# A mixture-of-experts layer: shared expert in 384 and 320 features, slot table turned one step sooner, last scatters awaited by SyncE

## The chip, the cores and the metric

The kernel runs on one core of a Trainium2 chip. The metric is the device time of one execution in microseconds (us). Three executions of the kernel before took 974.53, 976.37 and 980.57 us; the median is 976.37 us. One further execution was profiled, and all rows and times of engines come from it.

## What is computed

Inputs are x (4 x 512 tokens of 512 features), normalised per token to xn. Three things are added to x: an attention stand-in (projection, a scan over the tokens, projection), a routed mixture of experts and a shared expert:

```python
d = sigmoid(decay)
projected = xn @ W_in.T
state_t = d * state_(t-1) + (1 - d) * projected_t        # per sequence
attn = states @ W_out.T + bias

scores = softmax(xn @ wg_router.T)                        # 32 experts
topk_w, topk_idx = top_k(scores, 6);  topk_w /= sum(topk_w)
y  = sum over the 6 chosen e: topk_w * (silu(xn @ w_gate[e]) * (xn @ w_up[e])) @ w_down[e]   # F = 352
sh = (silu(xn @ ws_gate) * (xn @ ws_up)) @ ws_down                                            # 2F = 704
out = x + attn + y + sh
```

Matrix products are done to nearly float32 precision with three passes of TensorE: an operand is split into a high part (rounded to the fast format fp32r) and a low part (the rest), and hi*hi + hi*lo + lo*hi is accumulated.

## The kernel before, in words

**Units.** After the attention part, which ends at about 137 us, TensorE works through 40 units. Units 0 to 7 are the shared expert: SH = 8, two units for each of the four sequences, tokens() = 512. An even unit does features 0 to 351 of the shared expert, an odd one 352 to 703. Units 8 to 39 are the routed experts in order of load, with 448 down to 360 slots each. Every unit has three chunks of features, c = 0, 1, 2, of 128, 128 and 96 (FLAST). The order of TensorE in unit u is written out by hand: gate_up(u, 0), down(u-1, 2), gate_up(u, 1), down(u, 0), gate_up(u, 2), down(u, 1). A waiting instruction holds all that stands behind it on its engine.

**Cost of a chunk in matmuls.** For c = 0 and 1, gate and up are 4 slices of D times 3 passes each, so 24 matmuls. For c = 2 (gate_up_last), the first 64 gate and 64 up features stand in one 128-wide operand (WIDE_GU, 12 matmuls). The last 32 gate and 32 up features stand in another with their high and low parts side by side (w_nar, NARROW_GU), which needs only 2 passes: 8 matmuls (narrow). down is 3 matmuls for each of 4 blocks of tokens and each chunk, 12 per chunk. A shared unit has 24 + 24 + 20 + 36 = 104 matmuls, each 512 columns.

**ScalarE and VectorE** turn a chunk into the operand of down: silu (ScalarE), mult (VectorE), h_hi (ScalarE), h_lo (VectorE). For c = 2 it is silu, wide_h, and for the narrow part narrow_low (ScalarE), narrow_sum (VectorE), silu_narrow (ScalarE), narrow_h (VectorE) ahead of h_hi and h_lo. Three PSUM banks p_gu are used in turn. Weights come to raw (two halves), ScalarE writes the high part (w_hi_piece) and VectorE the low part (w_lo_piece), in pieces GATE, UP, WIDE_GU, NARROW_GU, DOWN, counted in s_wh and s_w.

**Slot table.** While units 0 to 5 run, GpSimd sends 96 small scatters (send, L582) that write which token has which slot of which expert. VectorE computes the places of choice k (choice_slots) in unit k-1. GpSimd then loads the table to tabrow (L593, L594). TensorE turns it (table_T, 4 small transposes) in unit 6 behind gate_up(6, 2). VectorE copies it out at the end of unit 6 (table_out, L1612 to L1616). Only then can GpSimd gather the tokens of units 8 and 9 (gather, L599). Their rows are rearranged by DMAs issued from SyncE and ScalarE (quarters, L369), transposed by VectorE (squares, L1571) and split (xt_hi, xt_lo) before unit 8's first matmul. ScalarE issues 8 of these DMAs in unit 7, between w_hi_piece(8, UP) and silu of chunk 1.

**Routed loop.** GpSimd gathers for unit u+2 once unit u+1's operand is split, then scatters unit u-1's result into out (scatter, L613). ScalarE evacuates y of unit u-1 (y_out) between pieces of unit u's work.

**End.** GpSimd issues the last three scatters, waits until all have landed (s_scat), reads a count (value_load, L641), branches over a loop for extra blocks that is not entered here, and meets the other engines at the end of the block (L123).

## Time and profile before

| what | value |
|---|---|
| median of three executions | 976.37 us (974.53 to 980.57) |
| the profiled execution, its own time | 976.6 us |
| its span, first to last instruction | 974.6 us |
| TensorE busy | 931.4 us (96% of the span) |
| VectorE, ScalarE, GpSimd busy | 651.6, 498.3, 516.9 us |
| mean granted clock of TensorE | 0.985 of 2.4 GHz |

The span is 2.0 us shorter than the execution's own time. Busy times of a matmul overlap with the next one's, because matmuls are pipelined: what a matmul costs in a stream is read from start to start.

### The profile page before, as it was taken

To read this page: it belongs to the slowest core of one execution; us is meant where nothing else is said; L and a number is where in the kernel's file an instruction comes from. 1 tells how busy PE (TensorE), PEld (TensorE's weight loads), DVE (VectorE), ACT (ScalarE), POOL (GpSimd) and SP (SyncE) were. 2 spreads that over 40 slices of the span, in tenths; PEclk is the share of its full clock that TensorE was granted. 3 is DMA by queue.
4 is the path that set the end of the run, shared out by engine and by line. 5 is a ranking of instruction groups with operands and counts; after the bars stand their busy time and mean duration, and the time that the engine had idled before them with its cause. 6 is when DMAs were issued, how large, how long until landed. Compare 5 with 4: busy or idle time off the path is not lost.

```text
span 974.6 us, 14045 instructions
## 1 busy us (share of the span) xinstructions
PE 931.4 (96%) x4596; PEld 836.7 (86%) x4596; DVE 651.6 (67%) x1098; ACT 498.3 (51%) x853; POOL 516.9 (53%) x376
## 2 busy tenths in 40 slices
PE   6899979999999999999999999999999999999992
PEld 6798868888888888899999999999999899989891
DVE  6789987454533676877667766776677667667650
ACT  5543224222222355766566756676566566566641
POOL 6210257777740435656665666566547547546341
PEclk9899989999999999999999999999999999999996
DMA  9506236130232559999998998989999989999842
GB/s 331 165 1 218 87 110 206 38 88 1 87 97 90 145 192 295 252 226 217 227 247 244 227 233 216 285 214 221 246 258 239 252 245 249 255 246 245 207 55 37
DMA packets 125834, 182.59 MB, mean 187 GB/s; under 512 B 19012, under 2 KB 72900, under 8 KB 125760
## 3 DMA queue, kind: packets, MB, share of 16 engines
q1 hardware_dynamic: 97840, 126.14, 41.7%
q0 software_dynamic: 26704, 55.01, 28.1%
q8 instruction: 38, 0.62, 0.3%
q10 hardware_dynamic: 1216, 0.53, 0.2%
q14 instruction: 36, 0.29, 0.1%
HBM read 114.21 MB, written 40.85 MB: 159 GB/s over the span
## 4 chain that ended last, share of the span: by engine, by line
PE 55%; DMA 11%; DVE 10%; SPq 8%; issue 7%; POOL 5%; ACT 3%; ACTq 1%; POOLq 0%; DVEq 0%
PE p_gu L961 10%; PE p_gu L962 10%; PE p_gu L963 10%; SPq L369 8%; DMA xnT<-xn_rows,ids 7%; PE p_y L961 6%; PE p_y L962 6%; PE p_y L963 6%; DMA xnT<-xnT 3%; POOL xnT L599 3%; POOL out L613 2%; DVE w_lo L1214 2%; PE p_gu L1045 2%; PE p_gu L1043 2%; DVE scan L1475 1%
## 5 line engine op out<-in xcount | busy, mean ns | idle before, releaser
L613 POOL DMA_INDIRECT out<-rows,ids x112 | 204.0, 1822 | 221.4 <-ACT rows L672 197.0
L961 PE MATMUL p_gu<-xT_hi,w_hi 128*128 128x512 f32 (+12 forms) x800 | 280.5, 351 | 0.6 <-DVE xT_lo L1214 0.6
L963 PE MATMUL p_gu<-xT_hi,w_lo 128*128 128x512 f32 (+12 forms) x800 | 280.4, 351 | 0.0
L962 PE MATMUL p_gu<-xT_lo,w_hi 128*128 128x512 f32 (+12 forms) x800 | 280.3, 350 | 0.0
L599 POOL DMA_INDIRECT xnT<-xn_rows,ids x112 | 164.5, 1468 | 88.6 <-issue 33.3
L1214 DVE TENSOR_TENSOR w_lo<-raw,w_hi 128x1024 fp32r<-128x1024 f32 (+2 forms) x134 | 161.3, 1205 | 0.5 <-ACT w_hi L672 0.5
L961 PEld LDWEIGHTS p_gu<-xT_hi,w_hi 128*128 128x128 f32 x800 | 150.2, 188 | 12.0 <-DVE xT_lo L1214 1.0
L962 PEld LDWEIGHTS p_gu<-xT_lo,w_hi 128*128 128x128 f32 x800 | 150.3, 188 | 10.9
L963 PEld LDWEIGHTS p_gu<-xT_hi,w_lo 128*128 128x128 f32 x800 | 150.3, 188 | 7.2
L961 PE MATMUL p_y<-w_hi,hT_hi 128*128 128x512 f32 (+1 forms) x384 | 151.5, 395 | 4.9 <-DVE hT_lo L1214 2.0
L962 PE MATMUL p_y<-w_lo,hT_hi 128*128 128x512 f32 (+1 forms) x384 | 150.5, 392 | 0.0
L963 PE MATMUL p_y<-w_hi,hT_lo 128*128 128x512 f32 (+1 forms) x384 | 150.2, 391 | 0.0
L672 ACT ACTIVATE w_hi<-raw 128x1024 fp32r<-128x1024 f32 (+2 forms) x136 | 142.6, 1051 | 7.6 <-PE p_y L963 6.3
L1420 DVE TENSOR_TENSOR h_sb<-sg,p_gu 128x512 f32<-128x512 f32 (+12 forms) x80 | 46.0, 574 | 127.3 <-PE p_gu L963 110.9
L582 POOL DMA_INDIRECT slot_table<-pay,slot_i x96 | 107.3, 1117 | 34.0 <-issue 27.7
L716 ACT ACTIVATE sg<-p_gu 128x512 f32<-128x512 f32 (+24 forms) x120 | 61.6, 513 | 120.2 <-PE p_gu L963 111.9
L672 ACT ACTIVATE hT_hi<-h_sb 128x384 fp32r<-128x384 f32 (+9 forms) x120 | 64.7, 540 | 112.5 <-DVE h_sb L1420 86.1
L1214 DVE TENSOR_TENSOR hT_lo<-h_sb,hT_hi 128x384 fp32r<-128x384 f32 (+9 forms) x120 | 68.9, 574 | 33.4 <-ACT hT_hi L672 32.8
L961 PEld LDWEIGHTS p_y<-w_hi,hT_hi 128*128 128x128 f32 (+1 forms) x384 | 72.1, 188 | 21.9 <-ACT rows L672 3.9
L1571 DVE STREAM_TRANSPOSE xT_raw<-xnT 128x512 f32<-128x512 f32 x112 | 72.9, 652 | 23.6 <-DMA xnT<-xnT 23.6
L672 ACT ACTIVATE xT_hi<-xT_raw 128x512 fp32r<-128x512 f32 (+3 forms) x112 | 64.9, 580 | 40.6 <-DVE xT_raw L1571 38.9
L963 PEld LDWEIGHTS p_y<-w_hi,hT_lo 128*128 128x128 f32 (+1 forms) x384 | 72.1, 188 | 15.7
(190 smaller groups left out, 1218.4 us busy)
## 6 DMA issues: line engine op xcount, KB each, us to landing
raw<-L_ffn_w_gate SPq DMA_DIRECT2D x32, 704.0 KB, 5.8
raw<-L_ffn_w_up SPq DMA_DIRECT2D x32, 704.0 KB, 7.8
xnT<-xnT SPq DMA_DIRECT2D x424, 48.0 KB
raw<-L_ffn_w_down SPq DMA_DIRECT2D x32, 512.0 KB
out<-rows SPq DMA_DIRECT2D x28, 256.0 KB, 3.3
xring<-L_attn_x SPq DMA_DIRECT2D x24, 256.0 KB, 3.6
raw<-L_ffn_w_down SPq DMA_DIRECT2D x32, 192.0 KB
xnT<-xnT SPq DMA_DIRECT2D x80, 64.0 KB
```

What stands on the lines that cost most here:

```text
L369: queue.dma_start(xq[par][a_ * SQ:(a_ + 1) * SQ, 0:n, b, :], xe[b * SQ:(b + 1) * SQ, 4 * par:4 * par + n, a_ * P:(a_ + 1) * P]).then_inc(s ...
L582: pool.indirect_dma_start(out=table[:, :], in_=pay[:, c, :], in_offset=None, out_offset=bass.IndirectOffsetOnAxis(ap=slot_i[:, c:c + 1], a ...
L599: pool.indirect_dma_start(out=xe[0:n, 4 * (u % 2) + t, :], out_offset=None, in_=xn_rows[:, :], in_offset=bass.IndirectOffsetOnAxis(ap=ids[ ...
L613: pool.indirect_dma_start(out=out[:, :], in_=y_sb[t][0:n, :], in_offset=None, out_offset=bass.IndirectOffsetOnAxis(ap=ids[0:n, col:col + 1 ...
L672: return a.activation(dst, src, ACT.Copy, scale=scale)
L716: a.activation(sg[0:k, 0:n], p_gu[2 * q % 3][0:k, 0:n], ACT.Silu).then_inc(s_sg, 1)
L961: t_.matmul(dst, stat[0], mov[0], start=first, stop=False)
L962: t_.matmul(dst, stat[0], mov[1], start=False, stop=False)
L963: return t_.matmul(dst, stat[1], mov[0], start=False, stop=last)
L1214: return v.tensor_tensor(dst, src, hi, ALU.subtract)
L1420: v.tensor_tensor(h_sb[0:k, 0:n], sg[0:k, 0:n], p_gu[(2 * q + 1) % 3][0:k, 0:n], ALU.mult).then_inc(s_h, 1)
L1571: v.transpose(xT_raw[u % 2][:, :, t * P:t * P + n].rearrange("p s (b j) -> p b s j", j=SQ), xq[u % 2][:, t, 0:n // SQ, :].rearrange("p b ( ...
```

## The change

The 704 features of the shared expert are cut into 384 and 320 instead of 352 and 352.

- An even unit has three full chunks of 128. Its chunk 2 has gate in one operand (in the place of WIDE_GU) and up in another: high part in w_nar[:, 0], low part in w_nar[:, 1]. It is 24 matmuls, and is followed by plain silu and mult.
- An odd unit has chunks of 128, 128 and 64. Its chunk 2 is WIDE_GU alone, 12 matmuls, then silu and wide_h. h_lo writes the low part of h to partitions 64 to 127 of hT_hi, under the high part, and the last 64 rows of ws_down are loaded twice, to partitions 0 to 63 and 64 to 127. down(u, 2) of an odd unit is then 2 matmuls per block: high and low part of h at once against the high weights, and the high part of h against the low weights.
- Set 0 of shared weights is 18 KB per partition in raw, so two scratch tiles move by 1 KB. One memset of raw and two waits on it go.
- table_T moves from behind gate_up(6, 2) to behind down(5, 2) in unit 6, and table_out on VectorE from the end of unit 6 to behind shared_out, ahead of the mult of chunk 1.
- GpSimd's wait for all scatters goes inside the branch that is not entered; SyncE waits for them as its last instruction.

The core of the diff (counters of semaphores, which follow from the above, are left out):

```diff
-KF = (P, P, FLAST)
+FS_EVEN = FC * P
+FS_ODD = 2 * F - FS_EVEN
...
+def width(u):
+    return F if u >= SH else (FS_EVEN, FS_ODD)[u % 2]
+def kf(q):
+    return min(P, width(q // 3) - q % 3 * P)
+def full_last(u):
+    return u < SH and u % 2 == 0
+def wide_only(u):
+    return u < SH and u % 2 == 1
...
             def shared_set(s):
...
+                down = shared_down(s).rearrange("p (c d) -> p c d", d=D)
+                sp.dma_start(down[:, 0:FC - 1, :],
+                             ws_down[a:a + FULL, :].rearrange("(c p) d -> p c d", p=P)
+                             ).then_inc(s_ld[2][0], 16)
+                for at_ in range(0, P, f - FULL):
+                    sp.dma_start(down[at_:at_ + f - FULL, FC - 1, :], ws_down[a + FULL:a + f, :]
+                                 ).then_inc(s_ld[2][0], 16)
...
             def gate_up_last(u):
...
                     mm = three(p_gu[2 * q % 3][:, 0:n], wide_pass(u % 2, kc),
                                [x_hi[:, kc, 0:n], x_lo[:, kc, 0:n]], kc == 0, kc == DC - 1)
+                if wide_only(u):
+                    mm.then_inc(s_ud, 1)
+                    return
                 mm.then_inc(s_gd, 1)
...
                 pe.wait_ge(s_sg, q)
+                if full_last(u):
+                    for kc in range(DC):
+                        mm = three(p_gu[(2 * q + 1) % 3][:, 0:n], [w_nar[:, i, kc, :] for i in range(2)],
+                                   [x_hi[:, kc, 0:n], x_lo[:, kc, 0:n]], kc == 0, kc == DC - 1)
+                    mm.then_inc(s_ud, 1)
+                    return
                 narrow(p_gu[(2 * q + 1) % 3], u % 2, (x_hi, x_lo), n).then_inc(s_ud, 1)
...
             def down(u, c):
...
+                    elif wide_only(u) and last:
+                        t_.matmul(p_y[t][:], hT_hi[:, q % 2, t * P:(t + 1) * P],
+                                  w_hi[:, u % 2, lo:lo + D], start=False, stop=False)
+                        mm = t_.matmul(p_y[t][:], hT_hi[0:k, q % 2, t * P:(t + 1) * P],
+                                       w_lo[0:k, u % 2, lo:lo + D], start=False, stop=True)
...
                 if u > 0:
                     down(u - 1, 2)
+                if u == SH - 2:
+                    table_T()
                 gate_up(u, 1)
                 down(u, 0)
                 gate_up(u, 2)
-                if u == SH - 2:
-                    table_T()
                 down(u, 1)
...
             def h_lo(q):
...
-                    low(hT_lo[0:k, q % 2, 0:n], h_sb[0:k, 0:n], hT_hi[0:k, q % 2, 0:n]
-                        ).then_inc(s_ht, 1)
+                    dst = hT_hi[WIDE:P] if k == WIDE else hT_lo[0:k]
+                    low(dst[:, q % 2, 0:n], h_sb[0:k, 0:n], hT_hi[0:k, q % 2, 0:n]).then_inc(s_ht, 1)
...
                         shared_out(t)
+                if u == SH - 2:
+                    table_out()
...
-                wide_h(u)
+                if full_last(u):
+                    mult(3 * u + 2)
+                else:
+                    wide_h(u)
                 if split is not None:
                     w_lo_piece(split, DOWN)
-                narrow_sum(u)
-                narrow_h(u)
+                if u >= SH:
+                    narrow_sum(u)
+                    narrow_h(u)
                 h_lo(3 * u + 2)
-                if u == SH - 2:
-                    table_out()
...
             scatter(UNITS - 1)
-            pool.wait_ge(s_scat, 16 * XB_ALL)
...
             more = pool.value_load(cnt_i[0:1, 0:1], min_val=0, max_val=XMAX)
             with pool.If(more > 0):
+                pool.wait_ge(s_scat, 16 * XB_ALL)
...
             more = sp.value_load(cnt_i[0:1, 0:1], min_val=0, max_val=XMAX)
             with sp.If(more > 0):
...
+            sp.wait_ge(s_scat, 16 * XB_ALL)
```

## Rows read from the trace of the kernel before

**Rows 1.** Busy time by stretch: TensorE, its weight loads, VectorE, ScalarE, GpSimd, granted clock.

```profile
core 0: us, PE busy (x) PEld busy (x) DVE busy (x) ACT busy (x) POOL busy (x), PEclk, DMA share, GB/s
137.00:336.00 199.00, 199.00 (x876) 164.02 (x874) 104.64 (x158) 55.96 (x82) 119.42 (x111) 1.00 0.34 100
336.00:650.00 314.00, 311.68 (x1544) 286.67 (x1544) 224.06 (x386) 196.53 (x363) 190.77 (x118) 1.00 0.89 232
...
765.00:912.00 147.00, 145.24 (x770) 133.92 (x769) 103.49 (x156) 93.13 (x155) 81.64 (x48) 1.00 0.97 251
```

**Rows 2.** Instructions in time, VectorE then TensorE, late in the routed units.

```profile
908.54 0.71 DVE L1571 STREAM_TRANSPOSE xT_raw<-xnT 128x512 f32<-128x512 f32 x1 [2.77 <-DMA xnT<-xnT]
...
911.59 0.47 PE L961 MATMUL p_y<-w_hi,hT_hi 128*128 128x512 f32 x1 [0.42 <-ACT rows L672]
```

**Rows 3.** TensorE in time, unit 1: its first matmul, narrow's first, unit 2's first.

```profile
169.42 0.39 PE L961 MATMUL p_gu<-xT_hi,w_hi 128*128 128x512 f32 x1
...
188.51 0.39 PE L1043 MATMUL p_gu<-xT_hi,w_nar 128*128 128x512 f32 x1
...
193.04 0.39 PE L961 MATMUL p_gu<-xT_hi,w_hi 128*128 128x512 f32 x1
```

**Rows 4.** TensorE in time around table_T and in units 7 and 8.

```profile
295.74 0.40 PE L961 MATMUL p_gu<-xT_hi,w_hi 128*128 128x512 f32 x1
...
308.47 0.26 PE L1142 MATMUL p_tx<-ident,tabrow 112*128 112x112 f32 x1
...
333.24 0.39 PE L961 MATMUL p_y<-w_hi,hT_hi 128*128 128x512 f32 x1
...
335.73 0.39 PE L963 MATMUL p_y<-w_hi,hT_lo 128*128 128x512 f32 x1
336.71 0.47 PE L961 MATMUL p_gu<-xT_hi,w_hi 128*128 128x448 f32 x1 [0.59 <-DVE xT_lo L1214]
...
342.60 0.50 PE L961 MATMUL p_y<-w_hi,hT_hi 96*128 96x512 f32 x1 [0.76 <-DVE hT_lo L1214]
...
351.15 0.47 PE L961 MATMUL p_y<-w_hi,hT_hi 128*128 128x512 f32 x1 [0.66 <-DVE rows L1603]
```

**Rows 5.** GpSimd in time: scatters of choices 4 and 5, load of the table.

```profile
235.31 0.98 POOL L582 DMA_INDIRECT slot_table<-pay,slot_i  x1 [1.80 <-DVE slot_i L1398]
...
258.93 0.98 POOL L582 DMA_INDIRECT slot_table<-pay,slot_i  x1 [1.19 <-DVE slot_i L1398]
...
283.31 0.63 POOL L593 DMA_DIRECT2D tabrow<-slot_table  x1 [3.32 <-DMA slot_table<-pay,slot_i]
283.93 0.59 POOL L594 DMA_DIRECT2D tabrow<-slot_table  x1
```

**Rows 6.** The tile tabrow: from issue to landing of its two loads.

```profile
DMA to landing us min/median/max: 5.4/5.7/6.1
```

**Rows 7.** Gathers, rearranging DMAs and silu in time: GpSimd, then ScalarE.

```profile
314.68 1.09 POOL L599 DMA_INDIRECT xnT<-xn_rows,ids  x1 [30.16 <-DVE wts L1616]
...
322.30 6.13 ACTq L369 DMA_DIRECT2D xnT<-xnT  x8
...
328.53 0.60 ACT L716 ACTIVATE sg<-p_gu 128x512 f32<-128x512 f32 x1 [8.20 <-issue]
```

**Rows 8.** VectorE in time: units 6 and 7.

```profile
301.46 0.69 DVE L1420 TENSOR_TENSOR h_sb<-sg,p_gu 128x512 f32<-128x512 f32 x1 [3.74 <-issue]
...
330.55 0.69 DVE L1214 TENSOR_TENSOR hT_lo<-h_sb,hT_hi 128x512 fp32r<-128x512 f32 x1 [0.70 <-ACT hT_hi L672]
...
335.66 0.99 DVE L1214 TENSOR_TENSOR xT_lo<-xT_raw,xT_hi 128x512 fp32r<-128x512 f32 x2
```

**Rows 9.** The end: GpSimd's last scatter, its read of the count, the block's end.

```profile
961.41 1.61 POOL L613 DMA_INDIRECT out<-rows,ids  x1 [0.30 <-issue]
...
L641 POOLq TENSOR_LOAD <-cnt_i x1: 516/516/516, 966.9 to 966.9; - x1
...
L123 SPq DRAIN  x1: 7/7/7, 921.1 to 921.1; - x1
...
L123 POOLq DRAIN  x1: 6358/6358/6358, 968.0 to 968.0; - x1
```

More of the change, by code:

```diff
@@ L348, in split_part, with from_raw, to_split @@
             return w[:, s, W_DOWN:W_ALL]
+        def from_raw(u, piece):
+            n = weight_set(u)
+            return shared_part(n, piece) if n < 2 else raw_part(raw_half(n), piece)
+        def to_split(w, u, piece):
+            if full_last(u) and piece == WIDE_GU:
+                return w[:, 0, W_WIDE:W_DOWN].rearrange("p (c f) -> p c f", c=DC)
+            if full_last(u) and piece == NARROW_GU:
+                return w_nar[:, 0 if w is w_hi else 1]
+            return split_part(w, u % 2, piece)
         def x_tile(t):
@@ L379, in tile_rows, with load_set @@
                 return dram[bass.ds(P * t, P), :]
-            def load_set(h, split, g_src, u_src, d_src):
+            def load_set(h, before, g_src, u_src, d_src):
                 for j, src in ((0, g_src), (1, u_src)):
-                    if split is not None:
-                        sp.wait_ge(s_w, split + NARROW_GU + 1)
+                    if before is not None:
+                        sp.wait_ge(s_w, split_done(before, DOWN) - 1)
                     lo, hi = PIECES[j]
@@ L387, in load_set @@
                                  ).then_inc(s_ld[j][h], 16)
-                if split is not None:
-                    sp.wait_ge(s_w, split + DOWN + 1)
+                if before is not None:
+                    sp.wait_ge(s_w, split_done(before, DOWN))
                 lo, hi = PIECES[2]
@@ L683, in w_hi_piece @@
                     act.wait_ge(s_dd if j == DOWN else s_ud, 3 * (u - 1))
-                copy(split_part(w_hi, u % 2, j), raw_part(half, j)).then_inc(s_wh, 1)
+                copy(to_split(w_hi, u, j), from_raw(u, j)).then_inc(s_wh, 1)
             def normalise(t):
@@ L712, in silu @@
                     act.wait_ge(s_pre, 64)
-                act.wait_ge(s_gd, q + 1)
+                u = q // 3
+                if wide_only(u) and q % 3 == FC - 1:
+                    act.wait_ge(s_ud, q + 1)
+                else:
+                    act.wait_ge(s_gd, gate_done(q))
                 act.wait_ge(s_h, q)
-                n, k = tokens(q // 3), (P, P, WIDE)[q % 3]
+                n, k = tokens(u), P if full_last(u) else (P, P, WIDE)[q % 3]
                 a.activation(sg[0:k, 0:n], p_gu[2 * q % 3][0:k, 0:n], ACT.Silu).then_inc(s_sg, 1)
@@ L731, in h_hi @@
                 act.wait_ge(s_h, q + 1)
[L732 to L734 removed]
+                if q % 3 == 2 and q >= 3 * SH:
+                    act.wait_ge(s_he, rank_of(q // 3) + 1)
+                n, k = tokens(q // 3), kf(q)
                 if ends_half(q // 3):
@@ L877, in _ @@
                 if split is not None:
-                    w_hi_piece(split, NARROW_GU)
+                    if not wide_only(split):
+                        w_hi_piece(split, NARROW_GU)
                     w_hi_piece(split, DOWN)
@@ L885, in _ @@
                 silu(3 * u + 2)
-                narrow_low(u)
-                silu_narrow(u)
+                if u >= SH:
+                    narrow_low(u)
+                    silu_narrow(u)
                 h_hi(3 * u + 2)
@@ L894, in _ @@
                 with act.Fori(0, more) as k:
-                    for j in range(3):
-                        act.wait_ge(s_ld[j][0], (2 if j == 2 else 1) * 16 * (k + raw_loads(E) + 1))
+                    for j in (0, 1):
+                        act.wait_ge(s_ld[j][0], 16 * (k + raw_loads(E) + 1))
+                    act.wait_ge(s_ld[2][0], 32 * k + 16 * (down_loads(E) + 2))
                     act.wait_ge(s_dd, 3 * k + 3 * UNITS)
@@ L1658, in _ @@
                     w_lo_piece(split, WIDE_GU)
-                    w_lo_piece(split, NARROW_GU)
+                    if not wide_only(split):
+                        w_lo_piece(split, NARROW_GU)
                 if early is not None and blocks(early) > 3:
```

138 lines of the change are left out of this document (85 added, 53 removed).

## The prediction

> **What bounds the kernel now.** I first read the table of busy time by stretch. From 137 to 336 us, the shared units, TensorE is busy in all of 199.00 us, at a granted clock of 1.00, while VectorE works 104.64 and ScalarE 55.96 us [rows 1]. So in this stretch time is the number of matmuls times their pitch, and other engines matter only where they make TensorE wait. In the routed units TensorE is idle for 2.32 us of 314 and 1.76 us of 147 [rows 1]: it is the bound there too, though late in the run only just. There the loop of gather, rearranging DMA and transpose is nearly as slow: VectorE stood 2.77 us before a transpose for a DMA, and 0.42 us of that kind of delay came through to TensorE [rows 2]. I then read TensorE in order of time for its pitch [rows 3] and for the places where it does stop [rows 4], then the producers behind those places [rows 5 to 8], and last the end [rows 9].
>
> **Fewer matmuls.** Unit 1 takes 193.04 - 169.42 = 23.62 us for 104 matmuls, so the pitch is 0.227 us [rows 3]. An even unit goes from 104 to 108 (chunk 2 from 12 + 8 to 24), an odd one to 92 (8 fewer in gate_up, 4 fewer in down). A pair saves 8, four pairs save 32: 32 x 0.227 = 7.27 us. Narrower operands cost the same: the pitch of unit 1 holds 96-row ones already. This is the term that I am surest of, since there is no idle time here to hide it.
>
> The row gives 0.227 us from start to start. The Trainium skill (TensorE: Matmul & The Clock Gate, Back-to-back issue gap) states about 131 ns per matmul as the sustained rate of a stream of weight loads and matmuls at 512 columns. The trace disagrees; by that figure 32 matmuls would be worth 4.2 us, and the forecast would be 3.1 us higher.
>
> **Is each operand ready for the earlier matmuls?** Shifts of TensorE against before, in matmuls: +4 behind gate_up(0, 2), -8 behind each whole pair; 24 (5.45 us) at the place of table_T in unit 6; 20 (4.54 us) in the first two chunks of unit 7; 28 (6.36 us) at the start of unit 8. The tightest place is chunk 1 of an odd unit, whose down comes 8 matmuls (1.8 us) sooner. In unit 7, where ScalarE is held by issuing DMAs, its hT_lo ended at 330.55 + 0.69 = 331.24 and down began at 333.24 [rows 4, 8], 2.0 us of margin; how it changes is worked out below. In other odd units ScalarE issues no DMAs, so their margin is larger. Behind chunk 2 the odd unit's down(u, 2) stands 24 matmuls later (5.4 us), and the chain there loses four instructions (narrow_low, narrow_sum, silu_narrow, narrow_h), while the even unit loses them too. I cost it at nothing. The split of set 0 has 256 columns more on each of the two engines and that of set 1 as many fewer: nothing, beside a busy TensorE. The removed memset and waits stand near the start, where GpSimd is not the bound: nothing, at most a few tenths.
>
> **The table turned sooner.** The 4 transposes are moved and not removed. TensorE reaches them at 295.74 - 5.45 = 290.3 [rows 4]. It then needs the table to have landed. Before, the loads were issued at 283.31 and 283.93 and took up to 6.1 us [rows 5, 6]: 290.0. GpSimd waited 1.80 and 1.19 us for choices 4 and 5 [rows 5], of which 0.30 stands before any scatter; VectorE comes to choice 4 sooner by 4 matmuls (0.9 us) and to choice 5 by 16 (3.6 us), but to choice 2 by 4 later. I take 1.5 us sooner for the load (bounds 0 and 2.4). The table lands near 288.5, 1.8 us before it is needed; at the bound of 0 the margin is 0.3. Behind table_T stands all of TensorE, so each microsecond of lateness would cost one: bounds 0 and 2 us, taken at 0. table_out now stands before mult of unit 6's chunk 1, where VectorE had been idle 3.74 us [rows 8]; its six small instructions fit. If that cover were gone, h of chunk 1 would be late.
>
> The first gather started at 314.68, after 30.16 us of waiting for the table's copy [rows 7]. It can start near 294, so tokens of units 8 and 9 are there long before they are asked for. What was late next: ScalarE was free at 328.53 - 8.20 = 320.33, stood until 322.30 for the gathers, and issued 8 DMAs in 6.13 us, and only then did silu [rows 7]. Now it issues from 320.33 - 4.54 = 315.8 to 321.9. From silu's start to the last xT_lo (336.65) was 8.12 us [rows 7, 8], so that one ends at 330.1. In the same way hT_lo of chunk 1 ends 2.71 us after silu's start, at 324.7, against a down at 333.24 - 6.36 = 326.9: no stop. TensorE reaches unit 8 at 336.71 - 0.75 - 6.36 = 329.6 (the 0.75 is 336.71 - 335.73 less a pitch [rows 4]) and waits 0.5 us. Gain 0.25 us (bounds -0.75, +0.75, by how long the 8 issues take).
>
> Next, down(7, 2) waited 0.76 us for hT_lo [rows 4], whose chain ran through the narrow steps behind the transposes; each took about as long as its neighbours (0.60 and 0.69 us [rows 7, 8]), so the chain is some 2.6 us shorter and the wait goes: gain 0.75 us (bounds 0 and 0.76). Then down(8, 0) waited 0.66 us for shared_out [rows 4], in VectorE's queue behind the transposes of unit 9. VectorE is less late now, but this queue is full: I take half, 0.3 us (bounds 0 and 0.66). After that everything is shifted alike. gather(10) waits for unit 8's operand and comes 6.5 us sooner, TensorE 8.6 us.
>
> **The end.** GpSimd's last scatter is done at 963.02. It waits for landing until 966.9, reads the count, and its DRAIN starts at 968.0 and takes 6.36 us: the kernel ends with it at 974.4 [rows 9]. In the changed kernel GpSimd doesn't wait. The 1.1 us from read to DRAIN start at 963.0, the DRAIN at 964.1, and it ends at 970.5, beside the landing instead of behind it. SyncE, idle since 921.1, sees the landing at 966.9 and its DRAIN is 7 ns [rows 9]. Gain 3.85 us, if the DRAIN's length is its own. No row shows a GpSimd DRAIN with DMAs in flight: bounds 0 (it counts from the landing, and the reading is not saved either) and 7.6 (it vanishes). I take the length in the row, since no DMA was in flight when it ran.
>
> That drain has a rule against it, which is the rival below. The Trainium skill (VectorE: DVE Perf Modes, The DRAIN you can't avoid) gives drains at a kernel's borders as about 12 ns on all engines. SyncE's 7 ns agrees, GpSimd's 6358 ns doesn't.
>
> **Sum.** 7.27 + 0.25 + 0.75 + 0.3 + 3.85 = 12.4 us. The profiled execution took 976.6 us (span 974.6), so **964.2 us** (span 962.2). The median of before, 976.37, is 0.2 us away: the sum holds for it too.
>
> **Rivals.**
> - *The drain starts anew at the landing.* For it: we don't know what 6.36 us consist of. Against: it ran when nothing was left to land. The end then gives 1.1 us (the reading) or 0: 967.0 to 968.0 us. Chance 0.17.
> - *The drain shrinks* to what SyncE's takes, and the end is the landing: 974.5 - 966.9 = 7.6 us from the end, 960.4 us. Chance 0.05.
> - *The gather loop takes over.* gather(10) comes only 6.5 us sooner against TensorE's 8.6. If the loop sets the late units, which VectorE's 2.77 us speak for and TensorE's 0.42 us against [rows 2], TensorE ends with 6.5 + 3.85: 966.2 us. Chance 0.12.
> - *The odd units don't get shorter*, because TensorE waits for h instead. Then the 16 matmuls that even units gain cost 3.6 us, and only the end is won: 976.4 us. The margin of 2 us at the tightest place [rows 4, 8] is against it. Chance 0.06.
> - *Slower: table_T holds TensorE.* It pays from a landing later than 290.3 us, one for one, and turns the sign 12.4 us later, at 302.7: a load of 20 us where 5.4 to 6.1 were seen [rows 6]. To be 1% slower it needs over 30 us. Chance 0.03, with anything else of this sign.
>
> **How the numbers follow.** My forecast has 0.57; the rivals have 0.43. About 1% is what a measurement of this kernel can tell from no change, that is 966.6 and 986.1 us. Faster by over 1%: the forecast 0.57, less 0.03 for its upper end, the shrunk drain 0.05, most of the loop case 0.09, and a little of the new-start drain 0.03: 0.71. Slower by over 1%: 0.03. Within: 0.26. The range goes down to 961.0 (the upper bounds of the start of unit 8 and a drain that starts during the last scatter) and up to 968.5, which takes in the loop case and the drain that starts anew, and leaves out the shrunk drain, the waiting odd units and the slower case, less than 0.2 together.
>
> **What would show it.** Right: 108 and 92 matmuls in shared units at a pitch of 0.227 us, no gap in TensorE between 137 us and unit 8, unit 8's first matmul near 330.2, table_T near 290.3 with no wait, the first gather near 294, TensorE's last matmuls some 8.6 us sooner, and GpSimd's DRAIN at about 6.4 us, starting before the scatters land. Wrong: a wait before table_T, a wait for hT_lo in units 1, 3, 5 or 7, longer gaps for rows after 765 us, or a DRAIN that ends as long after the landing as before.

## Result and the profile after

The changed kernel took 973.84 us (median of 20 executions, 969.61 to 980.05), the kernel before 976.29 us beside it (median of 20). The ratio is 0.9966, 95% interval 0.9951 to 0.9982: 2.45 us were won where 12.4 were forecast. The forecast of 964.2 us and its range (961.0 to 968.5) missed. The profiled execution took 976.52 us with a span of 974.8 us; that of before had 974.6. A single execution moves by 3 us and more, so times are taken from medians and places from profiles. Ratios compare the means of the executions that ran undisturbed, without those in a slower state, so a ratio and the quotient of two medians can differ by some tenths of a per cent.

**Down of the 64-feature chunk.** This is TensorE in order of time at the end of gate_up(5, 2) and through down(5, 2), which is directly ahead of table_T. Columns: start us, duration us, engine, line, operands, shapes, wait ahead. The operand that a weight load (PEld) puts into TensorE is here a block of hT_hi, not a weight of the model; both operands of such a matmul have the same number of rows. These eight matmuls are called a group below.

```profile
292.91 0.39 PE L1056 MATMUL p_gu<-xT_hi,w_lo 128*128 128x512 f32 x1
293.14 0.39 PE L1223 MATMUL p_y<-w_hi,hT_hi 128*128 128x512 f32 x1
293.45 0.50 PE L1225 MATMUL p_y<-w_lo,hT_hi 64*128 64x512 f32 x1
293.88 0.49 PE L1223 MATMUL p_y<-w_hi,hT_hi 128*128 128x512 f32 x1
294.31 0.50 PE L1225 MATMUL p_y<-w_lo,hT_hi 64*128 64x512 f32 x1
...
296.01 0.50 PE L1225 MATMUL p_y<-w_lo,hT_hi 64*128 64x512 f32 x1
296.44 0.37 PE L1254 MATMUL p_tx<-ident,tabrow 112*128 112x112 f32 x1
```

Up to 293.14 the pitch is the 0.227 us of [rows 3]. Then a matmul of 128 rows and one of 64 alternate, and each starts 0.43 us behind the last. Eight take 3.30 us instead of 1.81. No wait is shown ahead of any of them, and the clock did not fall during them, as the stretches below show. The weight loads (PEld) of the same stretch say what happens:

```profile
292.91 0.19 PEld L1223 LDWEIGHTS p_y<-w_hi,hT_hi 128*128 128x128 f32 x1
293.45 0.18 PEld L1225 LDWEIGHTS p_y<-w_lo,hT_hi 64*128 64x128 f32 x1 [0.35 <-issue]
293.88 0.19 PEld L1223 LDWEIGHTS p_y<-w_hi,hT_hi 128*128 128x128 f32 x1 [0.24 <-issue]
294.31 0.18 PEld L1225 LDWEIGHTS p_y<-w_lo,hT_hi 64*128 64x128 f32 x1 [0.24 <-issue]
```

The load for 293.14 was done under the matmul before it (292.91). From there on each load stands idle for 0.24 us and starts together with its own matmul: it no longer runs under the previous matmul. The waits of the weight loads over the whole run, in us, times and longest, show the same. The kernel before had four waits of this kind at p_y (3.3 us), as the changed kernel has at L1054; the other 28 are new:

```profile
PEld p_y L1225 <- issue: 4.3, 16, 0.4
...
PEld p_y L1054 <- issue: 4.1, 4, 1.6
...
PEld p_y L1223 <- issue: 2.9, 12, 0.2
```

**Clock.** The same stretches by window (columns as in [rows 1]: busy times, granted clock, DMA share, GB/s).

```profile
199.00:202.60 3.60, 3.60 (x11) 1.51 (x10) 2.38 (x4) 2.35 (x2) 2.92 (x3) 1.00 0.02 1
293.10:296.50 3.40, 3.40 (x10) 1.35 (x9) 2.41 (x4) 0.63 (x1) 0.00 (x0) 1.00 0.00 0
296.50:297.70 1.20, 1.20 (x5) 0.72 (x4) 1.20 (x3) 0.00 (x0) 0.00 (x0) 0.61 0.67 222
297.70:300.00 2.30, 2.30 (x6) 1.82 (x6) 1.33 (x7) 0.00 (x0) 0.12 (x1) 0.50 0.90 282
300.00:303.00 3.00, 3.00 (x8) 2.31 (x7) 0.00 (x0) 0.00 (x0) 2.39 (x3) 0.50 1.02 373
303.00:306.00 3.00, 3.00 (x13) 2.43 (x12) 0.00 (x0) 0.60 (x1) 2.39 (x3) 0.90 0.84 297
```

The slow groups run at 1.00. But behind this group and the four short transposes of table_T the clock is 0.50 (the 1.2 GHz level), and 13 matmuls run at 0.43 us, some 2.8 us lost. In the kernel before, nothing of the kind stood around table_T [rows 1, 4].

**Table and gathers, GpSimd.** The table is loaded at 283.81 and 284.43 (283.31 before [rows 5]), table_T starts at 296.44 with no wait, and the first gather is 14.8 us earlier than in [rows 7]:

```profile
283.81 0.63 POOL L678 DMA_DIRECT2D tabrow<-slot_table  x1 [2.48 <-DMA slot_table<-pay,slot_i]
284.43 0.59 POOL L679 DMA_DIRECT2D tabrow<-slot_table  x1
299.88 1.09 POOL L684 DMA_INDIRECT xnT<-xn_rows,ids  x1 [14.86 <-DVE wts L1727]
```

**Unit 8 and the routed loop.** All three waits of [rows 4] behind 335 us are gone, but unit 8 starts at 338.70, not near 330.2. TensorE there:

```profile
338.70 0.36 PE L1054 MATMUL p_gu<-xT_hi,w_hi 128*128 128x448 f32 x1
```

ScalarE in order of time at its first piece of unit 10's weights, in the kernel before:

```profile
364.76 1.06 ACT L672 ACTIVATE w_hi<-raw 128x1024 fp32r<-128x1024 f32 x1 [1.32 <-DMA raw<-L_ffn_w_gate]
```

The same piece after, then SyncE's queue, then TensorE, each in a fence of its own:

```profile
369.71 1.06 ACT L757 ACTIVATE w_hi<-raw 128x1024 fp32r<-128x1024 f32 x1 [5.67 <-DMA raw<-L_ffn_w_gate]
```

```profile
347.68 10.79 SPq L444 DMA_DIRECT2D xnT<-xnT  x16
358.51 2.21 SPq L547 DMA_DIRECT2D out<-rows  x4
362.12 0.36 SPq L461 DMA_DIRECT2D raw<-L_ffn_w_gate  x1
```

```profile
373.50 0.47 PE L1054 MATMUL p_y<-w_hi,hT_hi 128*128 128x512 f32 x1 [0.27 <-ACT rows L757]
...
376.39 0.50 PE L1054 MATMUL p_y<-w_hi,hT_hi 128*128 128x512 f32 x1 [1.26 <-ACT rows L757]
```

SyncE issues unit 10's weights behind 16 rearranging DMAs (10.79 us) and four stores. They come at 369.7, ScalarE stands for them 5.67 us (1.32 before) with its evacuations queued behind, and TensorE loses 1.5 us in two stops. TensorE had no stop here before.

**The end.** First GpSimd's last scatter, then, in the second fence, the lines of the block's end (count, duration in ns, start in us). SyncE's COMPARE_BRANCH carries its wait for the scatters, so its start, 969.9, marks their landing.

```profile
964.54 1.61 POOL L698 DMA_INDIRECT out<-rows,ids  x1 [0.30 <-issue]
```

```profile
L168 POOLq DRAIN  x1: 11561/11561/11561, 963.0 to 963.0; - x1
L168 SPq COMPARE_BRANCH  x1: 38/38/38, 969.9 to 969.9; - x1
L168 SPq DRAIN  x1: 67/67/67, 970.4 to 970.4; - x1
```

From the last scatter's end (966.15) to the DRAIN's end (974.56) are 8.41 us. Before they were 974.36 - 963.02 = 11.34 [rows 9]. So 2.9 us are won, not 3.85. The DRAIN ran from 963.0, beside the scatters, but it didn't end by itself: it took 11.56 us and ended 4.6 us behind the landing.

**A ledger.** Four stretches, each against the same stretch of before in the profiled executions: TensorE's first matmul of unit 0 (137.68 before), from there to unit 8 (199.03), from there to the last matmul (620.37), and on to the end of the span (17.5). The three kernels on the right are experiments, told of below. Each column is one execution, and that of the changed kernel was 2.7 us slower than its median; a stretch also moves by some 1 us between executions (the routed units of tail_only, an experiment that doesn't touch them, are 1.1 us shorter than before).

| us against before | forecast | after | full_rows_fifth | changed_early_load_again | full_rows_early_load |
|---|---|---|---|---|---|
| start of unit 0 | 0 | +1.4 | +2.9 | +4.0 | +3.5 |
| units 0 to 7 | -6.6 | +0.6 | -7.2 | -2.7 | -7.5 |
| routed units | -2.0 | +1.2 | +4.7 | -2.1 | -4.6 |
| end | -3.85 | -3.0 | -3.1 | -2.8 | -2.9 |
| span | -12.4 | +0.2 | -2.7 | -3.5 | -11.5 |

### The profile page after: what moved, and what is told of

Same layout as the page of the kernel before. It is cut to its first block, busy times and chain, and to the rows that moved or that the text cites. A ratio compares the mean times of both kernels' runs of the same rounds, so it can differ in the third digit from the quotient of the medians.

```text
span 974.8 us, 13932 instructions
## 1 busy us (share of the span) xinstructions
PE 936.7 (96%) x4564; PEld 836.8 (86%) x4564; DVE 641.8 (66%) x1081; ACT 488.6 (50%) x836; POOL 515.2 (53%) x375
## 4 chain that ended last, share of the span: by engine, by line
PE 68%; DVE 9%; DMA 6%; SPq 6%; issue 5%; POOL 3%; ACT 2%; ACTq 1%; POOLq 0%; DVEq 0%
PE p_gu L1054 13%; PE p_gu L1056 13%; PE p_gu L1055 13%; PE p_y L1054 7%; PE p_y L1055 7%; PE p_y L1056 7%; SPq L444 5%; DMA xnT<-xn_rows,ids 3%; DVE w_lo L1326 2%; DMA xnT<-xnT 2%; PE p_gu L1138 2%; POOL xnT L684 2%; PE p_gu L1136 2%; PE p_y L1040 1%; DVE scan L1586 1%
## 5 line engine op out<-in xcount | busy, mean ns | idle before, releaser
L1054 PE MATMUL p_gu<-xT_hi,w_hi 128*128 128x512 f32 (+12 forms) x800 | 282.2, 353 | 0.0
L684 POOL DMA_INDIRECT xnT<-xn_rows,ids x112 | 167.3, 1494 | 88.5 <-DVE xT_lo L1326 40.4
L1054 PEld LDWEIGHTS p_gu<-xT_hi,w_hi 128*128 128x128 f32 x800 | 151.0, 189 | 11.9 <-issue 0.7
L1531 DVE TENSOR_TENSOR h_sb<-sg,p_gu 128x512 f32<-128x512 f32 (+12 forms) x84 | 48.6, 579 | 158.2 <-PE p_gu L1056 144.4
L1054 PE MATMUL p_y<-w_hi,hT_hi 128*128 128x512 f32 (+1 forms) x368 | 144.7, 393 | 5.8 <-ACT rows L757 4.2
L757 ACT ACTIVATE w_hi<-raw 128x1024 fp32r<-128x1024 f32 (+2 forms) x136 | 142.6, 1050 | 11.9 <-PE p_y L1056 6.3
L1055 PE MATMUL p_y<-w_lo,hT_hi 128*128 128x512 f32 (+1 forms) x368 | 144.2, 392 | 0.0
L1056 PE MATMUL p_y<-w_hi,hT_lo 128*128 128x512 f32 (+1 forms) x368 | 144.0, 391 | 0.0
L805 ACT ACTIVATE sg<-p_gu 128x512 f32<-128x512 f32 (+23 forms) x120 | 61.7, 514 | 136.9 <-PE p_gu L1056 132.5
L757 ACT ACTIVATE hT_hi<-h_sb 128x384 fp32r<-128x384 f32 (+8 forms) x120 | 64.7, 539 | 124.8 <-DVE h_sb L1531 101.3
L1326 DVE TENSOR_TENSOR hT_lo<-h_sb,hT_hi 128x384 fp32r<-128x384 f32 (+8 forms) x116 | 66.2, 571 | 33.9 <-ACT hT_hi L757 32.7
L1054 PEld LDWEIGHTS p_y<-w_hi,hT_hi 128*128 128x128 f32 (+1 forms) x368 | 69.1, 188 | 21.4 <-ACT rows L757 4.2
L1056 PEld LDWEIGHTS p_y<-w_hi,hT_lo 128*128 128x128 f32 (+1 forms) x368 | 69.1, 188 | 14.9
```

What stands on the lines that cost most here:

```text
L684: pool.indirect_dma_start(out=xe[0:n, 4 * (u % 2) + t, :], out_offset=None, in_=xn_rows[:, :], in_offset=bass.IndirectOffsetOnAxis(ap=ids[ ...
L757: return a.activation(dst, src, ACT.Copy, scale=scale)
L805: a.activation(sg[0:k, 0:n], p_gu[2 * q % 3][0:k, 0:n], ACT.Silu).then_inc(s_sg, 1)
L1054: t_.matmul(dst, stat[0], mov[0], start=first, stop=False)
L1055: t_.matmul(dst, stat[0], mov[1], start=False, stop=False)
L1056: return t_.matmul(dst, stat[1], mov[0], start=False, stop=last)
```

## Experiments

My theory (A) after the two traces: a 64-row operand between 128-row ones stops the overlap of weight load and matmul, 1.5 us a pair. Rivals: two loads of the same tile hT_hi one after another are slow (B), or two passes into one bank with new weights each time are (C).

Each experiment ran beside the kernel before in one of five series. In three of them (those of full_rows, of full_rows_third and of changed_early_load) the kernel before had a median near 996 us and the others 983 to 995 (late_drain 1007), with TensorE standing between 200 and 300 us for nothing that the profile shows. I call these waits for instructions, though no run shows what was missing. There times say less and I go by the traces. The last section shows this wait.

### One operand at 128 rows

```diff
-                        mm = t_.matmul(p_y[t][:], hT_hi[0:k, q % 2, t * P:(t + 1) * P],
-                                       w_lo[0:k, u % 2, lo:lo + D], start=False, stop=True)
+                        mm = t_.matmul(p_y[t][:], hT_hi[:, q % 2, t * P:(t + 1) * P],
+                                       w_lo[:, u % 2, lo:lo + D], start=False, stop=True)
```

This adds the product of the two low parts; nothing is left out.

> The changed kernel, but the second matmul of an odd shared unit's last down chunk uses all 128 rows (high and low part of h against the low weights, which stand twice) instead of 64. Theory A, a 64-row matmul between 128-row ones can't have its weights loaded under its neighbour: the eight matmuls of down(u, 2) go back from a start-to-start of 0.43 to 0.227 us, 1.5 us per odd unit, 6 us in all, so TensorE reaches unit 8 some 6 us sooner and the time is near 968 us. Rival B, the two loads of the same tile hT_hi one after another are what is slow: the pitch stays at 0.43 us and the time at 974 us. Rival C, the two passes into one bank with new weights each time, at a lower clock: the granted clock in these stretches was 1.00, so nothing would change either.

Eight matmuls of down(u, 2) took 1.81 to 1.84 us. By these traces A holds: the order, the lines, the banks and the instructions ahead are the same, and only the rows differ. B and C fall. The time was 986.92 us beside 996.34, ratio 0.9929 [0.9885, 0.9973]. It can't show what the rows are worth, for the changed kernel did not run beside it, and in a later series of this kind that kernel had 0.9901 by itself.

rows_96 uses 96 rows (FLAST) in the same place, which adds the product of the low parts for 32 of the 64 features:

> As full_rows, but the second matmul uses 96 rows. It tells whether any change of the row count costs, or 64 rows alone. Any change: start-to-start 0.43 us in down(u, 2) of units 1, 3, 5, 7. 64 rows alone: 0.227 us, as the 96-row matmuls beside 128-row ones had in the kernel before.

The two kinds of row, TensorE in order of time, with a pitch of 0.234 us, 1.87 for eight:

```profile
201.41 0.39 PE L1223 MATMUL p_y<-w_hi,hT_hi 128*128 128x512 f32 x1
201.63 0.40 PE L1225 MATMUL p_y<-w_lo,hT_hi 96*128 96x512 f32 x1
201.87 0.40 PE L1223 MATMUL p_y<-w_hi,hT_hi 128*128 128x512 f32 x1
```

So it is not "fewer than 128 rows" as such. Between 96 and 64 something switches. One execution took 993.62 us beside 996.34.

grouped keeps the 64-row operands and changes the order, four matmuls of 128 rows and then four of 64:

```diff
+                if wide_only(u) and last:
+                    for t in range(blocks(u)):
+                        t_.matmul(p_y[t][:], hT_hi[:, ...], w_hi[:, ...], start=False, stop=False)
+                    for t in range(blocks(u)):
+                        t_.matmul(p_y[t][:], hT_hi[0:k, ...], w_lo[0:k, ...], start=False, stop=True)
```

> The changed kernel with 64-row matmuls kept, but down(u, 2) of an odd unit does the four 128-row matmuls first and then the four 64-row ones. Theory A (the switch costs, not the 64 rows): two switches, at the fifth matmul and behind the eighth, each about 0.2 us, the others at 0.227 us, so 1.1 us less per odd unit than in the changed kernel. If 64-row matmuls are slow by themselves, the last four stay at 0.43 us.

```profile
196.80 1.07 PE L1216 MATMUL p_y<-w_hi,hT_hi 128*128 128x512 f32 x4
197.79 1.20 PE L1219 MATMUL p_y<-w_lo,hT_hi 64*128 64x512 f32 x4
198.92 0.50 PE L1054 MATMUL p_gu<-xT_hi,w_hi 128*128 128x512 f32 x1
199.26 0.40 PE L1055 MATMUL p_gu<-xT_lo,w_hi 128*128 128x512 f32 x1
```

2.12 us from the first to unit 2's, against 3.30 alternating and 1.81 with full rows. The price belongs to the switch, not to the 64-row matmul. The matmul behind the last one of 64 rows starts its successor late too (199.26, 0.34 us on instead of 0.227), so the count has to go one matmul further. Nine starts then take 199.26 - 196.80 = 2.46 us instead of 2.04, 0.42 for two switches. Alternating takes 3.64 (199.27 to 202.91 in after), 1.6 for eight. Both ways a switch costs 0.2 us. One execution took 986.47 us. The Trainium skill (TensorEngine Tiling (Array Packing), Key Properties) states that changing the tiling mode drains TensorE, and its list of modes (Available Configurations) has one of 64 rows beside that of 128. These rows agree with it, if an operand of 64 rows is enough for another mode and one of 96 is not, which the page doesn't say and no run shows apart. It gives no price; these rows do.

### The parts of the change by themselves

tail_only is the kernel before with the wait for the scatters moved to SyncE. table_only is the kernel before with table_T and table_out moved ahead. split_only is the changed kernel with both of these undone.

```diff
-            pool.wait_ge(s_scat, 16 * XB_ALL)
+            sp.wait_ge(s_scat, 16 * XB_ALL)
```

> The kernel before with nothing changed but the end: GpSimd doesn't wait for the scatters, SyncE does. Theory D, the drain's time runs from something near the last scatter's issue: from the end of the last scatter instruction to the end of GpSimd's drain 8.4 us as in the changed kernel, against 11.3 before, so 2.9 us faster, 973.4 us. Rival E, a fixed length of 6.36 us that starts when GpSimd is through: 3.9 us faster. Rival F, the end is set by the landing plus 7.5 us as before: no gain.

Last scatter's end to end of DRAIN 8.6 us instead of 11.34, near theory D's 8.4. The time, 995.15 beside 996.34, ratio 0.996 [0.9904, 1.0016], agrees and can't show it alone.

```diff
+                if u == SH - 2:
+                    table_T()
                 gate_up(u, 2)
-                if u == SH - 2:
-                    table_T()
```

> The kernel before with table_T and table_out moved alone. Theory I: the gathers start some 18 us sooner, ScalarE issues its DMAs 2 us sooner in unit 7, and TensorE's wait at unit 8 (0.75 us) goes: up to 1 us faster, 0.1%. Rival J: the four transposes at the new place let the granted clock fall: half clock for 5 us behind them, 2 to 3 us slower.

973.58 beside 974.36, ratio 0.999 [0.9966, 1.0014]: nothing to be measured. In its profile TensorE had no stop from 137 to 760 us, and the clock behind table_T stayed at 1.00, so rival J falls.

> The change with table_T, table_out and the wait for the scatters left where they were before: only the split in 384 and 320. Theory A (mode switch): per pair 8 matmuls fewer (1.8 us) and 8 slow ones (1.5 us more), so 0.3 us per pair and 1.3 us in all, and some of the 0.8 us at down(7, 2): 1 to 2 us faster than before, no more than 0.2%. My forecast had 7.3 us for it.

977.43 beside 974.36, ratio 1.0003 [0.9977, 1.0028]. The eight matmuls took 3.31 us, and the clock stayed at 1.00 around table_T, which there comes 17 us behind a slow group. The split alone, 7.3 us in my sum, brought nothing that can be measured. Its profile has both sides of it: 2.7 us less from unit 0 to unit 8, and a unit 0 that starts 5.0 us later (142.64; see the last section). The three parts add up: +0.3, -1.0 and some -2.8 us for the end by the traces are -3.5; a ratio of 0.9966 is -3.3. With intervals of 2.4 us on either side of the first two, that is no more than agreement.

changed_again is the changed kernel in the same series:

> The changed kernel itself, beside the variants on the same chip. 0.3% faster than before, as measured first. down(u, 2) of units 1, 3, 5, 7 at 3.3 us for 8 matmuls. If the drop of the granted clock to half behind table_T (seen once, 2.8 us) belongs to the change, it is here again; if it was chance, not.

972.03 us, ratio 0.9968 [0.9946, 0.9991], as in the first measurement. Its profile is of an execution of 3262 us and says nothing on the places.

### The loads of unit 10 ahead of its rearranging DMAs

```diff
                 if t == TILES - TPB:
                     quarters(sp, SH, range(QUARTERS // 2))
                     quarters(sp, SH + 1)
+                    rank_set(2, SH)
                     quarters(sp, SH + 2)
...
-            rank_set(2, SH)
```

With the 128-row operands on top this was full_rows_early_load:

> full_rows, and in SyncE's queue the loads of unit 10's weights stand ahead of the rearranging DMAs of unit 10 instead of behind them and the last stores of the shared part. Theory G, ScalarE's 5.67 us wait for w_gate in unit 9 comes from that queue and costs TensorE its 2 us at 373 us: that wait goes, TensorE has no gap for y_out there, and the time is about 2 us under full_rows. Rival H, that gap only moves to the next unit, whose gathers are as late: no difference to full_rows. Against the kernel before: 8 us or 0.8% faster by G, 6 us by H.

964.87 us (six executions) beside 974.36, ratio 0.9883 [0.9852, 0.9913]. It beats the kernel before and the changed one. TensorE has no gap above 0.3 us from 345 to 865 us, and w_gate, issued at 328.05, is there long before ScalarE asks for it.

Which of the two edits brought it? Theory S says that the two costs add up, L that the late load is most of it. In one series I had all four combinations:

> The changed kernel, its 64-row operands kept, with SyncE's loads of routed unit 10's weights moved ahead of the quarters of unit 10, as in full_rows_early_load. Theory S (two costs that add up: the 64-row operands some 4 to 6 us over the four pairs, the late w_gate up to 2 us): no ScalarE wait on raw near 370, 1 to 2 us under changed_fourth, 4 to 6 us above full_rows_early_load. Theory L (the late load is most of it): within 1.5 us of full_rows_early_load.

> The changed kernel with the four 64-row operands of each pair at 128 rows, nothing else. Theory S: 1.5 us less for each of four groups of eight matmuls, 6 us in all less what the waits behind take back, so 4 to 6 us under changed_fourth and 1 to 2 us above full_rows_early_load; the ScalarE wait on raw near 370 is there. Theory L: within 1.5 us of changed_fourth.

> Both edits, beside each of them alone. Theory S: the lowest of the four, 6 to 8 us under changed_fourth, some 10 us under the kernel before. Theory L: the same as changed_early_load.

> The changed kernel, for its time and profile beside the other three. 2 to 3 us under the kernel before. Down(u,2) of odd units 3.3 us for 8 matmuls. Open: whether the granted clock falls behind table_T's transposes (some 2.8 us lost) as it did in the profile of the changed kernel; a second profile without issue stalls tells whether that belongs to the kernel or to one execution.

| beside 996.72 us | w_gate as in the change | early |
|---|---|---|
| 64-row operands | 988.54, 0.9901 [0.9863, 0.9939] | 982.90, 0.9863 [0.9820, 0.9907] |
| 128 rows | 986.67, 0.9884 [0.9845, 0.9922] | 982.75, 0.9858 [0.9815, 0.9901] |

Here the early load was worth 5.6 and 3.9 us and the operands 1.9 and 0.15. Each kernel has six or seven executions, spread over 6 to 10 us: by their means only the early load with 64-row operands stands just clear of noise (4.3 us, give or take 3.7), the other three differences don't. In the traces the groups took 3.31 and 1.81 us as always, but TensorE stood for instructions in the shared units, and from the start of unit 0 to unit 8 were 209.9 us with 64 rows and 211.3 with 128 (both with the early load), where full_rows_early_load had 191.6 before. That a TensorE that is faster there only reaches that wait sooner is my reading and not shown. So two of them once more, and this time without that wait:

> The changed kernel with 128-row operands alone. Where TensorE waits for instructions between 220 and 300 us, that wait swallows the difference: 2 us at most against the changed kernel (986.67 and 988.54 in the call before). Where it doesn't (the kernel before near 975), theory S: 1.5 us for each of the three groups ahead of unit 8 and no clock fall behind table_T give 4 to 6 us, so 966 to 970, and the late w_gate leaves it 1 to 4 us above full_rows_early_load. Theory L (the late load is most of the loss): 970 or more.

> The 64-row operands kept, w_gate loaded early. Where TensorE waits for instructions: 4 us or more under the changed kernel, like full_rows_early_load (both 983 in the call before). Where it doesn't, theory S: 971 to 973, the 64-row groups and the clock fall behind table_T still there. Theory L: 966 to 968.

971.43 us, ratio 0.9941 [0.9919, 0.9964], and 971.90, ratio 0.9947 [0.9923, 0.9972], beside 977.02. The first lies a little above theory S's 966 to 970, the second within its 971 to 973, and L's 966 to 968 for the second falls. With 0.9966 for neither and 0.9883 for both, measured in other series, either edit alone brings about 0.002 and both 0.008. But the intervals of the single edits reach down to nothing, and the 0.004 by which both together exceed the two single gains is less than its own interval (0.005, worked out from the intervals of the four ratios). In the series with all four it didn't show: 0.9901 without and 0.9858 with both. So the times show that both together help, 8.5 us of the means beside changed_again and 4.7 beside changed_fourth. They don't show how the gain is shared. That the two costs hide each other rests on the traces. In the ledger 128 rows win 7.7 us up to unit 8 (2.8 of it the clock), and the routed units give 3.5 back, although their own group is 1.5 us shorter. ScalarE of full_rows_fifth, then its TensorE, then its windows:

```profile
364.79 1.06 ACT L757 ACTIVATE w_hi<-raw 128x1024 fp32r<-128x1024 f32 x1 [8.25 <-DMA raw<-L_ffn_w_gate]
```

```profile
368.58 0.47 PE L1054 MATMUL p_y<-w_hi,hT_hi 128*128 128x512 f32 x1 [2.85 <-ACT rows L757]
...
371.48 0.79 PE L1054 MATMUL p_y<-w_hi,hT_hi 128*128 128x512 f32 x1 [1.11 <-ACT rows L757]
```

```profile
371.40:374.00 2.60, 2.52 (x6) 2.04 (x7) 2.40 (x5) 2.60 (x8) 2.15 (x2) 0.50 1.12 261
374.00:377.00 3.00, 3.00 (x10) 2.68 (x10) 1.86 (x6) 1.47 (x2) 2.54 (x2) 0.55 1.24 176
```

TensorE came 6.3 us sooner to unit 8, the weights 4.9 us sooner than in after: the wait grew from 5.67 to 8.25 us, TensorE lost 4 us in two stops, and the clock fell behind them for some 5 us. With the early load ScalarE does this piece at 363.27 in changed_early_load_again, with no wait ahead.

### Table late with fast matmuls, and the drain

> The changed kernel with 128 rows in the 64-feature operands, beside its sibling with the table turned late, on one chip. Theory (64-row weights beside 128-row ones cost the first 1.5 us in each pair): 8 matmuls of down(u,2) take 1.8 us, no clock drop behind table_T (296 to 303 us at 1.00), time 966 to 970 where the kernel before has 974 to 976, of which the split gives 4 x 1.8 = 7.3 less the later start of unit 0, and the end gives 2.7. The w_hi piece of unit 10 still waits for w_gate (TensorE loses up to 2 us near 375): that part is what the earlier load of full_rows_early_load took away. Rival (the early load made all the difference there): 972 or more here.

> full_rows with table_T and table_out back behind down(u,2) of unit 6, so late that gathers begin near 312. Theory T (the move is worth what unit 8 waits for rows): 0.6 us at the start of unit 8 and up to 1.1 us in its first down chunks come back, 1 to 2 us longer than full_rows_third. Rival N (the pairs' gain makes the gathers late): unit 8 could start 5 us sooner, near 331, while its tile comes from gathers that begin no sooner than 312 and take 20 us to a transposed tile, so TensorE waits 1 to 5 us ahead of unit 8; 2 to 5 us longer. Rival Z (the table's place is worth nothing): same time within 0.5 us, no wait ahead of unit 8.

> The changed kernel once more, for its profile beside full_rows_third on one chip. Theory (64-row weights): down(u,2) 3.3 us for 8 matmuls, time 3.5 to 6 us above full_rows_third. Open is whether the clock falls again behind table_T: if the eight slow matmuls with the four short transposes behind them bring it about, the stretch from table_T's start on for 8 us has a granted clock of 0.5 to 0.9 again and about 2.8 us are lost; if the fall was a chance of one execution, it shows 1.00 and unit 8 starts 2 us sooner against unit 0 than in the profile of the changed kernel.

990.13, 990.83 and 991.04 us, where the kernel before had a median of 996.55 and ran from 976.05 to 1005.56 in the same series. Nothing on time follows. In the trace of full_rows_late_table the gathers began at 328.00, 12.5 us later than in full_rows_third; unit 8 had no wait, so rival N falls. But down(8, 0) waited 1.19 us for shared_out, and TensorE's first stop behind w_gate was 0.6 us shorter. What the move is worth isn't shown: from unit 8 to the last matmul this profile is 2.5 us shorter than that of full_rows_third.

late_drain puts 8 clears between the landing and the read of the count on GpSimd, in the kernel before:

```diff
             pool.wait_ge(s_scat, 16 * XB_ALL)
+            for i in range(8):
+                g.memset(scratch[:, 1, :], 0.0).then_inc(s_pool0, 1)
+                pool.wait_ge(s_pool0, 7 + i)
```

> The kernel before with eight clears of 512 bytes a row on GpSimd, one after the other, between the landing of the last scatters and the read of the count. Whether GpSimd's drain at the end is a fixed length or an end time counted from the last scatter. Theory F (fixed length): the drain still takes 6.36 us, and its end moves by all that the clears take (2 to 5 us). Theory E (it ends a given time after the scatters): the drain gets shorter by what the clears take, its end 11.3 us behind the last scatter's end as in the kernel before.

GpSimd in order of time, and in the second fence its DRAIN:

```profile
987.51 1.62 POOL L613 DMA_INDIRECT out<-rows,ids  x1 [0.30 <-issue]
992.88 4.60 POOL L637 MEMSET scratch<- 128x512 f32 x8 [3.75 <-DMA out<-rows,ids]
```

```profile
L123 POOLq DRAIN  x1: 6358/6358/6358, 998.5 to 998.5; - x1
```

The same 6358 ns, and all is over 4.4 us later against the last scatter. Behind a landing the length is fixed (F). With scatters in flight it is another, and the traces tell what it hangs on. In all 16 with the moved wait, that of changed_again included, the DRAIN ended 4.63 us behind the landing, to 0.01 us. Behind the last scatter's end it was 7.8 to 8.8 us, because the landing took 3.2 to 4.1, and the length itself was 8.0 to 12.0 us. So its end follows the landing, and not the last scatter and not its own start.

## Why the prediction was wrong, point by point

- **Failed step: "Narrower operands cost the same: the pitch of unit 1 holds 96-row ones already."** That row bears on 96 rows, and rows_96 confirms it (0.234 us). The changed kernel has 64, which no row of before showed in a stream. The step was an extrapolation told as a reading. It costs 4 x 1.5 = 6 us of the 7.27; 24 slow matmuls and 4.5 us of it stand ahead of unit 8. The trace of before did hold a hint, in table_T, whose second and fourth transpose have 64 rows:

```profile
309.22 0.33 PE L1144 MATMUL p_tx<-ident,tabrow 64*128 64x64 f32 x1
309.48 0.50 PE L961 MATMUL p_y<-w_hi,hT_hi 128*128 128x512 f32 x1
309.82 0.40 PE L962 MATMUL p_y<-w_lo,hT_hi 128*128 128x512 f32 x1
```

The matmul behind the 64-row one holds the next up for 0.34 us instead of 0.227, the same as behind a group.
- **The clock, which I did not weigh.** Behind a slow group with table_T's transposes it was 0.50 for some 6 us and cost 2.8 in after's profile. The profiles of changed_third and changed_early_load showed it too, the latter for half as long; those of changed_fourth and changed_early_load_again did not. None of the seven profiles with 96 or 128 rows and table_T behind them did, nor grouped's, nor table_only's. So it came only where an alternating group and table_T stand together, and there in three of five: neither alone was seen to bring it about, and what decides it is open.
- **Unit 8's start**, forecast 330.2, measured 338.70. The 8.5 us are 1.4 of a later unit 0, 4.5 of three slow groups and 2.8 of the clock, less some tenths. Without slow groups it was right: full_rows_fifth needs 191.88 us from unit 0 to unit 8, I had 192.5.
- **Operands ready for the earlier matmuls:** right in this profile. No stop for hT_lo in units 1, 3, 5 or 7. In the series with waits for instructions eight profiles have such a stop of 0.6 to 3.7 us between 240 and 305 us, so the margin holds only without those waits. The waits at unit 8, down(7, 2) and down(8, 0) are gone, 2.0 us in all where I had 1.3.
- **The table:** no wait, but loaded at 283.8, not 1.5 us sooner. TensorE's gain wasn't there, so it did not matter. The first gather came at 299.88 instead of 294, by the same 6 us as table_T.
- **The gather loop (0.12):** not what happened, though near it. It is not the gathers that hold the routed units but SyncE's queue, in which unit 10's weights stand behind 16 rearranging DMAs; I had looked for what is late next on ScalarE and VectorE only. It costs 1.5 us in after, and it would have taken about 4 of the gain even with the operands at 128 rows: full_rows_fifth, 971.43 us, misses the forecast too.
- **The end:** 2.9 us where I had 3.85. The reading of the count is saved, as forecast. The DRAIN's length is not its own: with scatters in flight it ends 4.63 us behind the landing, in every trace. That is my rival "starts anew at the landing" in kind, with 4.63 in place of 6.36, and the 1.1 us of the reading and this difference of 1.7 make 2.8.
- **Not foreseen: a later unit 0.** See below.

Together, in the profiled execution: 7.2 us in the shared units (4.5 and 2.8), 3.2 in the routed ones (1.5 for the fourth group, 1.5 for w_gate), 0.9 at the end and 1.4 of a later unit 0 are, but for roundings, the 12.6 us between forecast and measured span. By the medians 10 us are missing.

With 128 rows and the early load most of the sum I made is there: 964.87 us, 9.5 us under the kernel before in its series, and the profiled span 11.5 us shorter. It isn't there term by term (unit 0 starts 3.5 us later, the routed loop wins 2.6 more), so that the number is nearly the forecast's is in part luck.

## What to carry to other kernels

Don't put operands of 64 rows between ones of 128: each switch cost 0.2 us, beside a pitch of 0.227. Pad to full rows, or group them, and where a forecast says "costs the same" ask whether a row shows this very shape. When TensorE gets faster ahead of a loop, follow every queue of its loads, the DMA issuer's too: of a gain of 7.7 us, 4 went at one load that stood behind 16 issues. Where two edits each stay below the noise (0.2% here) and the traces say that one uncovers the other's cost, test them together before dropping either: together they were 0.5 to 0.9% under the changed kernel.

## What the runs showed of the hardware

**A clock fall ahead of the change.** In 10 of 15 profiles with the split (all but changed_again's) the granted clock fell behind the router's short matmuls, long before the shared units, and unit 0 began at 139.1 to 142.6 us; in the other five at 136.5 to 138.0. In four profiles without it (before, tail_only, table_only, late_drain) there was no fall and 136.5 to 137.7. First the kernel before, then after:

```profile
68.00:71.00 3.00, 3.00 (x21) 2.73 (x21) 2.63 (x5) 0.02 (x1) 0.00 (x0) 1.00 0.02 5
```

```profile
66.00:68.00 2.00, 2.00 (x20) 2.00 (x19) 2.00 (x5) 0.00 (x0) 0.00 (x0) 1.00 0.00 0
68.00:71.00 3.00, 3.00 (x11) 2.61 (x11) 1.80 (x3) 0.41 (x1) 0.00 (x0) 0.51 0.02 5
```

The 10 with the fall have a mean of 141.0 us, the 5 without it 136.9. Why the split should bring it about, where it changes nothing on TensorE at that place, is open, and so is whether it does: it may be chance. The times of the kernel before come in two groups as well. In the series of split_only 19 of its executions have a mean granted clock of 0.985 to 0.987 and a median of 974.1 us, 10 have 0.980 to 0.984 and 979.0 us. So a loss of this size is not the split's alone, though no profile shows where the slower ones of before have theirs.

**Waits for instructions, as I call them.** TensorE in full_rows_fourth, in the middle of gate_up, and the stretch as a whole by window:

```profile
229.25 0.58 PE L1055 MATMUL p_gu<-xT_lo,w_hi 128*128 128x512 f32 x1 [1.74 <-issue]
```

```profile
222.00:240.00 18.00, 10.98 (x31) 7.00 (x29) 2.27 (x4) 1.71 (x3) 9.77 (x10) 0.66 0.02 2
```

For 18 us nothing in the profile is waited for, TensorE works 61% of the time, and the clock falls as well (0.66). It came in three series of five, in kernels with and without the change, and made some 20 us in the kernel before (996 against 974 to 977) and some 16 in the changed one (988.5 against 972). Its cause isn't settled. While it was there, what 128 rows save in the shared units could not be seen in the time.
